# Moving the steps at which DVE, POOL and ACT prepare what PE reads, in a hand-ordered attention and expert kernel

## What is computed

```python
x = x + attn(layernorm(x))          # retention layer
x = x + ffn(layernorm(x))           # softmax attention and experts

def attn(x):                        # q, k get rotary phases, decay per head
    out = (q @ k.T / sqrt(8) * decay) @ v
    return groupnorm(out) @ Wo.T

def ffn(x):
    h = rms(x) * n1_w
    q, k, v = rms(h @ wq.T) * qn_w, rms(h @ wk.T) * kn_w, h @ wv.T
    x = x + softmax(causal(q @ k.T / sqrt(8))) @ v @ wo.T
    xf = rms(x) * n2_w
    w = top2(softmax(xf @ gate_w.T))
    o0 = gelu(xf @ up0) @ down0
    o1 = (silu(xf @ w1) * (xf @ w2)) @ down1
    o2 = gelu(gelu(gelu(xf @ l1) @ l2) @ l3) @ l4
    o3 = gelu(gelu(xf @ d3) @ u3) @ out3
    return x + w[0] * o0 + w[1] * o1 + w[2] * o2 + w[3] * o3
```

## Time and profile before

| | |
|---|---|
| median of 3 runs | 1111.49 us (1104.63 to 1120.81) |
| profiled execution | 1106.94 us |
| its span, first to last instruction | 1105.2 us |
| mean granted clock of PE | 0.805 |

### The profile page before, as it was taken

How to read it: one execution, slowest core, us unless ns; L and a number is a source line. 1 busy time by engine, 2 the same in 40 slices (tenths; PEclk the granted TensorE clock), 3 DMA queues, 4 the chain that set the end, 5 groups by cost and what they waited for, 6 DMA issues and landing times.

```text
span 1105.2 us, 16378 instructions
## 1 busy us (share of the span) xinstructions
PE 916.0 (83%) x6192; PEld 544.2 (49%) x6192; DVE 512.6 (46%) x1123; ACT 522.6 (47%) x1072; POOL 371.5 (34%) x595
## 2 busy tenths in 40 slices
PE   2656788889889888998889978988888889899767
PEld 1535544554546454465446454645545354444434
DVE  2334555455653664366544674376426542443021
ACT  1426235335645464464545554546445256333624
POOL 5334143215412642145313641264215231320311
PEclk9677666667789986997889897988699669757859
DMA  4000000000000000000000000000000000000000
GB/s 147 1 10 1 1 10 2 1 2 10 1 1 2 20 1 1 1 21 1 1 1 1 20 1 1 2 11 1 1 1 12 0 2 1 10 2 1 10 0 10
DMA packets 13724, 9.04 MB, mean 8 GB/s; under 512 B 2128, under 2 KB 13136, under 8 KB 13648
## 3 DMA queue, kind: packets, MB, share of 16 engines
q1 hardware_dynamic: 13648, 8.00, 2.5%
HBM read 5.64 MB, written 2.10 MB: 7 GB/s over the span
## 4 chain that ended last, share of the span: by engine, by line
PE 57%; DVE 13%; POOL 11%; ACT 9%; issue 8%; DMA 1%; SPq 0%; POOLq 0%; ACTq 0%; DVEq 0%
PE side L472 13%; PE outs L409 8%; PE side L358 7%; DVE mneg L874 6%; PE scores L389 5%; PE maxima L371 4%; PE outs L448 4%; PE side L509 4%; PE maxima L374 4%; PE side L455 3%; PE side L429 3%; ACT p L654 3%; POOL z L1131 2%; POOL p L1095 2%; POOL hA L1177 2%
## 5 line engine op out<-in xcount | busy, mean ns | idle before, releaser
L874 DVE TENSOR_REDUCE mneg<-maxima 128x2 f32<-128x256 f32 (+3 forms) x256 | 211.1, 824 | 302.6 <-PE maxima L374 300.6
L654 ACT ACTIVATE p<-scores 128x1024 f32<-128x1024 f32 (+3 forms) x256 | 180.6, 705 | 158.8 <-PE scores L389 158.0
L1095 POOL TENSOR_SCALAR_AFFINE_SELECT p<-p 128x256 f32<-128x256 f32 x256 | 105.8, 415 | 410.7 <-ACT p L654 409.5
L371 PE MATMUL maxima<-ks,qs 24*128 24x384 f32 (+3 forms) x512 | 107.4, 416 | 51.0 <-DVE mneg L874 50.1
L389 PE MATMUL scores<-qs,ks 25*128 25x256 f32 (+3 forms) x512 | 121.8, 472 | 29.2 <-ACT p L654 28.5
L409 PE MATMUL outs<-p,v2x 128*32 128x512 f32 (+3 forms) x1024 | 115.1, 581 | 4.0 <-POOL p L1095 4.0
L389 PEld LDWEIGHTS scores<-qs,ks 25*128 25x128 f32 x512 | 54.9, 211 | 106.3 <-ACT p L654 57.7
L1103 POOL TENSOR_SCALAR_AFFINE_SELECT p<-p 128x512 f32<-128x512 f32 x64 | 40.8, 637 | 161.1 <-ACT p L663 161.1
L371 PEld LDWEIGHTS maxima<-ks,qs 24*128 24x128 f32 x512 | 58.3, 225 | 73.6 <-DVE mneg L874 71.2
L884 DVE TENSOR_TENSOR p<-side,sb_t_tri 128x512 f32<-128x512 f32 x64 | 44.2, 690 | 104.4 <-PE side L429 104.4
L374 PE MATMUL maxima<-negb,idb 128*128 128x128 bf16 x512 | 82.1, 249 | 0.0
(11 more groups left out here) (154 smaller groups left out, 1517.4 us busy)
## 6 DMA issues: line engine op xcount, KB each, us to landing
x_in<-x_dram SPq DMA_DIRECT2D x8, 256.0 KB, 2.9
qs<-mT SPq DMA_DIRECT2D x128, 2.0 KB
out_dram<-yout SPq DMA_DIRECT2D x8, 256.0 KB, 2.3
sb_t_cos<-t_cos_dram SPq DMA_DIRECT2D x1, 512.0 KB, 4.9
sb_t_sin<-t_sin_dram SPq DMA_DIRECT2D x1, 512.0 KB, 5.1
sb_w_l<-w_l_dram SPq DMA_DIRECT2D x2, 256.0 KB
sb_w_qkv<-w_qkv_dram SPq DMA_DIRECT2D x2, 192.0 KB, 3.5
sb_w_u<-w_u_dram SPq DMA_DIRECT2D x3, 128.0 KB
```

Of the source, the lines that this page charges most:

```text
L371: nc.tensor.matmul(mb[:, i, 0:n + 128], qs[rows, b % 2, g, n:n + 128], ks[rows, b % 2, g, 0:n + 128], start=True, stop=False, skip_group_c ...
L654: A_(p2[kt][:, 2 * hp:2 * hp + 2, :], eb[:, :, 0:n], ACT.Exp, scale=float(D) ** -0.5).then_inc(exp_done, 1)
L874: V.tensor_reduce(mneg[:, g, 2 * hp:2 * hp + 2, qt], mb[:, :, 0:128 * (qt + 1)], AX.X, ALU.max, negate=True)\
L1095: Q.affine_select(out=diag, in_=diag, compare_op=ALU.is_ge, fill=0.0, base=0, pattern=[[0, 2], [1, 128]], channel_multiplier=-1).then_inc( ...
```

## The change

Nothing is computed in another way; operations get other steps and places.
- z leaves step 10. POOL makes it in the expert block of the next iteration, two operations after the masks of place 2 and two in place 6. Since its inputs (`mv`, `ry_pre`) then stay in use for longer, DVE waits at step 9 and POOL at step 10 for the z of the batch before, and `z_ready` counts four.
- `nat` goes to step 12, H to 14, Q20 to Q23 to 15 to 18.
- norm2: squares at 17 and 19, sums at 19 and 21, `halving` at 22, `newton` at 23, products with k at 24 and with q at 25; POOL's weighting of q at 25, the `high` copies at 26 and 27, the low parts at 27. The copy of v (`v2x`) on POOL goes from 19 to 21.
- The transposes of k go to steps 28 and 30, the first half of q's to 31, and the second half (S202, S203) to place 0 of the next iteration, after the first two units of retention scores.
- N20 and DVE's work on it go to step 10; N21 stays at 20. DVE copies the first output half in place 1 ahead of the experts' product, not at the end.
- At places 2, 4 and 6 PE does the experts' matmuls ahead of `retain`.
- The squares of y, their root, `nat2`, XF, GATE and the logits come one step later each (25, 26, 28, 29, 30, 31).

```diff
 SIDE_UNITS = {
-    0: [(1, "SC00"), (1, "SC01"), (-2, "G0"), (-2, "U0"), (1, "SC02"), (1, "SC03")],
+    0: [(1, "SC00"), (1, "SC01"), (0, "S202"), (0, "S203"), (-2, "G0"), (-2, "U0"), (1, "SC02"), (1, "SC03")],
...
-    NF + 10: [(2, "Q11")],
+    NF + 10: [(2, "Q11"), (-1, "N20")],
...
-    NF + 13: [(1, "H")],
-    NF + 14: [(1, "Q20")],
-    NF + 15: [(1, "Q21"), (2, "QT")],
-    NF + 16: [(1, "Q22"), (2, "ST")],
-    NF + 17: [(1, "Q23"), (0, "MT1")],
-    NF + 18: [(2, "S100"), (2, "S101")],
+    NF + 14: [(1, "H")],
+    NF + 15: [(1, "Q20"), (2, "QT")],
+    NF + 16: [(1, "Q21"), (2, "ST")],
+    NF + 17: [(1, "Q22"), (0, "MT1")],
+    NF + 18: [(1, "Q23"), (2, "S100"), (2, "S101")],
...
-    NF + 20: [(2, "S110"), (2, "S111"), (-1, "N20"), (-1, "N21")],
+    NF + 20: [(2, "S110"), (2, "S111"), (-1, "N21")],
...
-    NF + 24: [(1, "S210"), (1, "S211")],
-    NF + 25: [(1, "S212"), (1, "S213"), (0, "MT2")],
-    NF + 28: [(-1, "XF")],
-    NF + 29: [(-1, "GATE")],
-    NF + 30: [(1, "S200"), (1, "S201")],
-    NF + 31: [(1, "S202"), (1, "S203")],
+    NF + 25: [(0, "MT2")],
+    NF + 28: [(1, "S210"), (1, "S211")],
+    NF + 29: [(-1, "XF")],
+    NF + 30: [(1, "S212"), (1, "S213"), (-1, "GATE")],
+    NF + 31: [(1, "S200"), (1, "S201")],
 }
-SPLIT2_AT = {24: (1, 0), 25: (1, 2), 30: (0, 0), 31: (0, 2)}
+SPLIT2_AT = {28: (1, 0), 30: (1, 2), 31: (0, 0), 32: (0, 2)}
...
-        z_ready = counted("z_ready")
+        z_ready = counted("z_ready", NT)
...
-                    for x in range(2):
-                        dst = side(f"N2{x}", b)
-                        pe.wait_ge(oT_ready, count(oT_ready, b, x + 1))
-                        transposed(dst, lambda t: oT[:, x, t * 128:(t + 1) * 128])
+                if s in (10, 20):
+                    x = (s - 10) // 10
+                    dst = side(f"N2{x}", b)
+                    pe.wait_ge(oT_ready, count(oT_ready, b, x + 1))
+                    transposed(dst, lambda t: oT[:, x, t * 128:(t + 1) * 128])
...
                     if t is None:
+                        if on(it - 2):
+                            experts(it - 2, place)
                         if place in (2, 4, 6, 7) and on(it + 1):
                             retain(it + 1, {2: 0, 4: 1, 6: 2, 7: 3}[place])
-                        if on(it - 2):
-                            experts(it - 2, place)
                     else:
                         if on(it + 1):
                             retained_scores(it + 1, t, (0, 1))
+                        if place == 0 and on(it):
+                            before(it, G * GK)
                         if on(it - 2):
...
-                if s == 22:
+                if s == 26:
                     act.wait_ge(k2_normed, count(k2_normed, b, 1))
                     high(1).then_inc(high2_ready, 1)
-                if s == 23:
+                if s == 27:
                     act.wait_ge(q2_weighted, count(q2_weighted, b, 1))
                     high(0).then_inc(high2_ready, 1)
...
                         unmasked(it + 1, t, 1)
+                    if place == 0 and on(it):
+                        before(it, G * GK)
                     if on(it - 2):
...
                     dve.wait_ge(x1_ready, count(x1_ready, b, 1))
+                    if b:
+                        dve.wait_ge(z_ready, count(z_ready, b, 0))
                     moments(x1[:, b % 3], 1)
...
-                if s == 11:
+                if s == 12:
                     dve.wait_ge(root_ready["pre"], count(root_ready["pre"], b, 1))
...
                 rv, _, ry, _ = scratch["norm2"]
-                if s == 18:
-                    for m in range(2):
-                        dve.wait_ge(sq2_ready, count(sq2_ready, b, m + 1))
-                        i = V.tensor_reduce(red2[:, 64 * m:64 * m + 64],
...
-                    step(i)
-                    step(V.tensor_scalar(rv[:], red2[:], 1.0 / D, EPS_RMS, ALU.mult, ALU.add))
-                if s == 19:
+                if s in (19, 21):
+                    m = (s - 19) // 2
+                    dve.wait_ge(sq2_ready, count(sq2_ready, b, m + 1))
...
+                    if m:
+                        step(i)
+                        step(V.tensor_scalar(rv[:], red2[:], 1.0 / D, EPS_RMS, ALU.mult, ALU.add))
+                if s == 22:
                     halving("norm2")
-                if s == 20:
+                if s == 23:
                     newton("norm2")
                     newton("norm2")
-                if s == 21:
-                    if on(b + 1):
+                if s in (24, 25):
+                    if s == 24 and on(b + 1):
                         dve.wait_ge(low1_ready, count(low1_ready, b + 1, 4))
-                    for n in (1, 0):
+                    for n in (25 - s,):
                         V.tensor_tensor(qk[:, n].rearrange("p t (h d) -> p t h d", d=D),
...
                             .then_inc((q2_normed, k2_normed)[n], 1)
-                if s == 23:
+                if s == 27:
...
-                if s == 20:
-                    for x in range(2):
-                        src = side(f"N2{x}", b)[:].rearrange("p (a e) -> p a e", e=2 * D)
...
+                if s in (10, 20):
+                    x = (s - 10) // 10
+                    src = side(f"N2{x}", b)[:].rearrange("p (a e) -> p a e", e=2 * D)
+                    step(V.reciprocal(rcp[:, x, :], src[:, :, D]))
...
-                if s == 27:
+                if s == 28:
                     dve.wait_ge(root_ready["tail"], count(root_ready["tail"], b, 1))
...
                     t = {0: 0, 1: 1, 3: 2, 5: 3}.get(place)
                     if t is not None and on(it + 1):
                         masked(it + 1, t, 0)
+                    if place == 1 and on(it - 1):
+                        take_output(it - 1, 0)
                     if on(it - 2):
                         experts(it - 2, place)
                     if t is not None and on(it + 1):
                         masked(it + 1, t, 2)
-                    if place == 1 and on(it - 1):
-                        take_output(it - 1, 0)
...
             def before(b, s):
                 if s == 10:
+                    if b:
+                        pool.wait_ge(z_ready, count(z_ready, b, 0))
                     root(b, "pre")
                     pool.wait_ge(root_ready["pre"], count(root_ready["pre"], b, 1))
-                    if b >= 3:
+                if s in (G * GK + 2, G * GK + 6):
+                    if s == G * GK + 2 and b >= 3:
                         pool.wait_ge(ysq_ready, count(ysq_ready, b - 3, 1))
                         pool.wait_ge(xf_ready, count(xf_ready, b - 3, 1))
-                    for t in range(NT):
-                        i = Q.tensor_scalar(z[:, b % 3, t, :], x1[:, b % 3, t, :], mv[:, 1, t, 0:1], scratch["pre"][1][:, t:t + 1],
-                                            ALU.subtract, ALU.mult)
-                    i.then_inc(z_ready, 1)
-                if s in (16, 18):
-                    m = (s - 16) // 2
+                    for t in (0, 1) if s == G * GK + 2 else (2, 3):
+                        Q.tensor_scalar(z[:, b % 3, t, :], x1[:, b % 3, t, :], mv[:, 1, t, 0:1], scratch["pre"][1][:, t:t + 1],
+                                        ALU.subtract, ALU.mult).then_inc(z_ready, 1)
+                if s in (17, 19):
+                    m = (s - 17) // 2
                     if on(b + 1):
                         pool.wait_ge(qk1_ready, count(qk1_ready, b + 1, 1))
...
                     Q.tensor_tensor(sq[:, tt, :], raw[:, tt, :], raw[:, tt, :], ALU.mult).then_inc(sq2_ready, 1)
-                if s == 21:
+                if s == 25:
...
-                if s == 23:
+                if s == 27:
                     pool.wait_ge(high2_ready, count(high2_ready, b, 2))
                     low(0, low2_q)
-                if s == 19:
+                if s == 21:
...
+                    if on(it):
+                        before(it, G * GK + place)
```

More of the change, by code:

```diff
@@ L1027, in tail @@
                     take_output(b, 1)
-                if s == 20:
-                    for x in range(2):
-                        src = side(f"N2{x}", b)[:].rearrange("p (a e) -> p a e", e=2 * D)
-                        step(V.reciprocal(rcp[:, x, :], src[:, :, D]))
-                        V.tensor_tensor(nat2[:, :, 64 * x:64 * x + 64].rearrange("p t (s d) -> p t s d", d=D),
-                                        src[:, :, 0:D].rearrange("p (t s) d -> p t s d", t=NT),
-                                        bc(rcp[:, x, :].rearrange("p (t s) -> p t s", t=NT), D), ALU.mult).then_inc(n2_read, 1)
+                if s in (10, 20):
+                    x = (s - 10) // 10
+                    src = side(f"N2{x}", b)[:].rearrange("p (a e) -> p a e", e=2 * D)
+                    step(V.reciprocal(rcp[:, x, :], src[:, :, D]))
+                    V.tensor_tensor(nat2[:, :, 64 * x:64 * x + 64].rearrange("p t (s d) -> p t s d", d=D),
```

(4 more changed lines are left out.)

33 lines of the change are left out of this document (17 added, 16 removed).

## The result

The changed kernel takes **1045.84 us** (median of 4 runs, 1044.05 to 1049.64), the kernel before beside it 1116.15 us (4 runs, 1104.63 to 1122.06): a ratio of 0.9407 [0.9316, 0.9498]. The forecast was 1061 in a range of 1022 to 1100. The profiled execution of the changed kernel took 1049.64 us (span 1047.9, mean granted clock 0.813, before 0.805). Between the medians the gain is 70 us, between the profiled executions 57: that of before (1106.94) was 9 us under the median here, that of the changed kernel 4 above its own.

What follows compares the result with a forecast made beforehand. PE's own queue sets the pace, with its waits and low clock to win. Terms of 1.6, 2.1, 0.9, 1.2 and 1.3 make 7.1 us a round, 48 in all: 1061 us, range 1022 to 1100.

Steps and rivals of the forecast that it cites:

- the period: Sign of being right: the period of the regular iterations comes out near 112 us, from 119.3 before.
- the mean granted clock: Sign of being right: PE's mean granted clock over the run, 0.805 before, comes out near 0.83.
- the five regular rounds: Iterations 1 to 5: 7.1 us of 119.3 saved in each, 35.5 us together.
- Step 13: Steps 9 to 15: shorter waits on DVE and POOL save 1.6 us a round, the regained clock 2.1.
- the price I put back at step 15: New wait at step 15 behind DVE's second sine pair: 1.0 us, bounds 0 and 2.6.
- Norm2, XF and the transposes: Steps 17 to 31: norm2's spacing saves 0.9 us a round, covering XF and moving the transposes 1.2.
- the first rival: Thin steps 26 to place 1 fall to 1.2 GHz, winning below clock 0.61: 1147 us, chance 0.10.
- The expert block: Waits for the output copy (1.4) and gelu (0.9) hidden, less 1.0 for moved copies: 1.3 us a round.
- Round -1: Iteration -1: z's 3.90 us no longer stand between POOL's root and cosine product, saving 3.5 us.
- Rounds 0, 6 and 7: Iterations 0 and 6 have about half a regular round's gain, 7 us; iteration 7 saves 2 us.
- The second: Waits and low clock return at steps 14 to 16 and 24 to 25: 1089 us, chance 0.25.
- The third rival: Clock regained wholly at step 13 and for half the loss from 777 to 803 us: 1027 us, chance 0.18.

Runs made afterwards that it cites:

- the second run: The changed kernel unaltered, run again on another chip: 1057.22 us, ratio 0.9427 to the kernel before.
- The spread: Changed kernel with norm2's squares at steps 17 and 18, sums 19 and 20, halving 21, Newton 22 and 23: 1052.8 us, then 1037.06 beside the changed kernel.
- the halves: POOL's cosine product in two halves, at steps 12 and 13, added to the kernel with norm2 spread over steps 19 to 23: 1045.05 us, ratio 0.9262.
- the fillers: 24 unused transposes of the identity on PE at steps 24, 26 and 27; alone in the changed kernel: 1039.72, 1058.08, 1062.38 and 1056.02 us, no ratio.
- the last kernel above: Changed kernel with norm2 spread, cosine product in two halves and unused identity transposes at steps 24, 26 and 27 together: 1018.46 us, ratio 0.9118.

## Why the prediction came out

The time lay 15 us under the forecast and inside its own range. The gain was sized too low: 57 us in place of 48 between profiled executions, 70 between the medians and 60 in the second run. Over the whole span PE is not busy for 160 us in place of 189, and its busy time fell by 28: about half of the gain is waits and half is clock, where the sum had 5.0 of waits and 2.1 of clock in a round. Of the signs named, the period came to 111.3 in the mean (named: near 112), the mean granted clock to 0.813 only (named: 0.83). Of the 57, the five regular rounds gave 42.4, predicted 35.5. Term by term for the last regular round, 9.95 us against 7.1:

**Step 13: 4.3, predicted 3.7.** The removed waits (2.00 and 0.56) went, for the reason given, and the price I put back at step 15 was named rightly and sized too low: 1.83 us in place of 1.0. So the waits gave 0.7, not 1.6. The clock gave the rest: the stretch went from 0.78 to 0.98. It is worth 4.3 - 0.7 = 3.6, near the upper bound of 4.3 where I had taken the middle, 2.1. The lower clock didn't go, it got shorter: it now follows the new wait of 1.83, at 0.73 where 0.55 followed the old ones, and lies mostly past the border, in steps 16 to 18:

```profile
701.17:707.50 6.33, 6.29 (x30) 3.80 (x30) 1.65 (x2) 4.45 (x10) 2.94 (x5) 0.73 0.00 0
```

**Norm2, XF and the transposes: 3.4 - 1.25 = 2.2, predicted 2.1.** Steps 16 to 21 gave 3.4: the wait of 2.3 vanished, and the clock rose from 0.86 to 0.91. The wait of 0.6 at step 23 did not go. PE waits 0.69 there, and with 0.74 and 0.92 at the next two steps that makes 2.35 us at the Newton operations, where I had 1.5; so of 2.9 us of waits norm2 gave 0.6, not 1.4. XF's 1.5 went. But steps 22 to 31 lost: what XF brought, and more, the clock of 0.56 from 721 to 741 took. That is the first rival's mechanism in its place and below its deciding clock of 0.61, though it ends with XF and doesn't reach place 1: from step 31 on the clock is 1.00. So the sum of these steps came out by luck: a larger gain before step 22 and a loss behind it, which is not in the sum. The spread took steps 22 to 30 from 24.5 to 21.2 us, and with the halves and the fillers they took 19.0 at best: 3.3 to 5.5 us a round still lay there.

**The expert block: 3.45 at equal work, predicted 1.3.** Both waits went (2.3; 2.6 by the run with the old order). PE's idle time there fell from 3.0 to 1.8 only, since 1.0 on silu and 0.8 on DVE's reading of GATE are new; this last I had bounded by 1.23. The 1.0 that I subtracted for the copies of S202 and S203 was not there: the run with them put back moved by 0.2. The rest of the gain is the clock, 1.00 for 0.94, which I had not counted here at all.

**Round -1: predicted 3.5, came 1.2.** This is the step that failed. z is off POOL's path, and the wait of 4.56 us that PE had there for the sum with the cosine product is gone; but the product, no longer behind z, now runs beside `nat` and holds it up. PE's two waits before and the window of the round, then DVE, POOL, PE and the window in the changed kernel:

```profile
78.17 0.63 PE L358 MATMUL side<-sb_t_id,nat 128*128 128x128 f32 x4 [2.17 <-DVE nat L964]
...
85.69 1.08 PE L358 MATMUL side<-sb_t_id,hA 128*128 128x128 f32 x4 [4.56 <-POOL hA L1177]
...
60.95:126.56 65.61, 40.84 (x318) 32.13 (x318) 26.63 (x74) 26.08 (x56) 24.52 (x26) 0.74 0.02 5
```

```profile
77.22 3.23 DVE L968 TENSOR_SCALAR nat<-x,mv,ry_pre 128x128 f32<-128x128 f32 x4 [0.62 <-POOL ry_pre L1126]
...
77.27 2.34 POOL L1179 TENSOR_TENSOR hA<-h,sb_t_cos 128x1024 f32<-128x1024 f32 x1
...
80.60 0.63 PE L356 MATMUL side<-sb_t_id,nat 128*128 128x128 f32 x4 [4.09 <-DVE nat L968]
...
61.32:125.72 64.40, 42.21 (x318) 32.21 (x318) 28.97 (x74) 26.06 (x56) 23.76 (x26) 0.71 0.02 5
```

The transposes of `nat` wait 4.09 us, where they waited 2.17 before: 1.9 of the 4.56 are lost to the meeting. PE is not busy for 22.2 us in place of 24.8, but at a clock of 0.71 in place of 0.74, and so 1.2 is left. Rounds 0, 6 and 7, 9 in the forecast, came to 14.0: 7.1 for round 0 and 6.9 from the last copy to the end. In the latter PE's idle time fell only from 43.7 to 42.6 us, and the rest is the clock (0.75 to 0.78), which fell to 0.74 there in the run with z back; so most of this 6.9 can't be put down to the change.

**The rivals.** The second (the waits only move) was half right: at step 13, 1.83 of 2.56 us came back two steps later, and in norm2 2.35 of 2.9. Its low clock moved with the wait, too, and what it missed is that the lower clock got shorter on the way. The Trainium skill's sentence that was weighed with it (TensorE: Matmul & The Clock Gate, A second HAM failure mode: psum-queue depth-cycling: short idles of PE make the clock swing) agrees with the trace at steps 23 to 28, where waits of 0.50 to 1.06 us stand by a clock of 0.56, and behind step 15. It doesn't give the price: behind the same wait of 1.82 us the same steps took 15.06 us or 19.44, and in the last kernel above, behind waits of 1.28 and 0.62 us at steps 14 and 15, the clock stayed at 1.00. The third rival's first half, the clock wholly regained at step 13, nearly came within steps 9 to 15; its second half came only with the spread and the fillers, in the later runs.

**What stays open** is what tips the clock. In the last kernel above the rounds from 561 and from 671 us take the same 15.2 and 14.4 us at 1.00 in steps 9 to 21, and then one falls to 0.61 and the other holds 1.00. No run here told the two apart.

## What to carry to other kernels

Follow a wait of the busiest engine back through the queue of the engine that releases it: here no operation was made faster, and the cure was one or two steps between the instruction that produces and the one that consumes, with work of another kind in between. Then look at what now runs at the same time as what: two operations that met by being moved gave back 1.8 of 2.6 us in one place and 1.9 of 4.6 in another. And where the busiest engine's clock falls in a thin stretch, the waits can be the small part of the price; try to spread them, or to fill them, though here the fillers lost in two rounds of five. Compare whole runs, since one kernel's own rounds differ by several us.

## What had not been expected of the hardware

The same transposes and matmuls of steps 22 to 30 take 19.0 us at a granted clock of 1.00 or 26.3 us at 0.61, in one execution, with PE idle for 1.8 us in the shorter and 0.7 in the longer.

POOL's cosine product holds up DVE's sine pair (0.75 to 2.64 us) and `nat` (1.11 to 3.06 and 3.23), but not DVE's reduction (1.23 us beside it). The pair of 2.64 us ends 0.83 us after the product does, about the time that it takes alone, as if most of it had begun only then. POOL's z does not hold the pair up: beside z it took 0.84. The Trainium skill (SBUF — State Buffer, SBUF: two separate sides) describes DVE and GpSimd as sharing a port pair that one of them holds for a whole instruction. The product beside `nat` and the pair agrees with that, z beside the pair doesn't; the runs show no reason for the difference.
